# Two orders changed on VectorE: the third residual tile against a norm, and two maxima against a sum

## The chip, the cores and the metric

One core of one Trainium2 chip runs the whole program. The metric is the time on the device in microseconds (us), the median of repeated runs. A separate execution was recorded by the hardware profiler; all rows below come from it.

The names of the engines in the rows: PE is TensorE's matmul and PEld its weight load, DVE is VectorE, ACT is ScalarE, POOL is GpSimd, and SPq is the queue in which SyncE issues DMAs.

## The reference

A transformer block over x of shape (16, 512, 512): 16 batches, 512 tokens, width 512.

```python
x = x + attn(layernorm(x))     # mLSTM, 8 heads of 64 values, 32 queries/keys each
x = x + ffn(layernorm(x))      # w1, w2 made ternary, gelu, 512 -> 2048 -> 512

# one mLSTM step per head (a scan over the tokens)
m_new = max(f_log + m, i_t);  F = exp(f_log + m - m_new);  I = exp(i_t - m_new)
C = F * C + (I * k_t) v_t^T;  n = F * n + I * k_t
h = (q_t C) / (max(|q_t n|, exp(-m_new)) + EPS)
# then a norm of h over each head's 64 values, * gamma, * sigmoid(o), @ Wout.T
```

The denominator is what the second edit touches: the larger of |q n| and exp(-m), which is the larger of the three numbers q n, -q n and exp(-m).

## The kernel before

The tokens of a batch are cut into T = 4 tiles (for the scan: chunks) of 128. The scan is computed chunk by chunk: within a chunk as a masked product of scores and values, across chunks by a carried state. Matmul operands are split into a high and a low float16 part, so a product takes two or three matmuls.

**Stages.** One stage of the program, `sequence(b, fb, ahead)` on each engine, holds the attention part of batch b, the feed-forward part of batch fb = b - 1, the start of batch b + 1 (its gate product and the first values) and the first norm of batch b + 2. Every engine has its own list of instructions in program order, written out by hand; what ties the lists together are semaphores. An instruction that waits holds up all that stand behind it on its engine.

**TensorE's order at the end of a stage** (L2107 to L2137): the last quarters of the feed-forward product `down` (L1997) alternate with the output projections `project(b, t)` of the four tiles (L1840, pa<-wT,shared). After tile 2's projection come the gate product of batch b + 1 (`gates`, L1807), its first values product (`tokens`, L1840, pa<-wT,xT), and then tile 3's projection. Next come the other values products into psh, the key features (L1816), the gate columns (`gate_columns`, L1848: four small transposes that wait for ScalarE's last gate exponential, L879) and the query features. The two banks of PSUM tile `pa` are used in turn; each use waits until the one two before it has been read. The values product takes the bank that the residual of tile 2 has read; tile 3's projection takes the one that the gate sum has read.

**VectorE's order at the end of a stage** (L1623 to L1671): `head_stats` of the four chunks, with the feed-forward results (L1538) between them; the statistics of x(b+2) (`next_stats`, L1260 and L1245 to L1266); the gating of chunk 3 (L1477); and then the residuals. `residual(b, t)` adds the projection to x (L1488) and takes statistics of the sum (L1491). `next_norm` applies the norm to tiles of x(b+2) (L1271), which ScalarE and VectorE split into parts only in the next stage. `gate_sum` (L1297), `gate_minus` and `gate_logs` work on the gates of b + 1: ScalarE and VectorE take turns on them, up to ScalarE's exponentials L878 and L879.

**`head_stats(b, j, ch)`** copies the chunk's products out of PSUM (L1437 in chunk 0, L1443 in the others), makes the denominators `den` in two maxima (L1445, L1450) and two further steps (L1453, L1457), and subtracts each head's mean (sum over columns L1447, scaled by L1451, subtracted by L1455). It then gates chunk j - 1 (L1477), sums the squares that ScalarE has made (L983, L1462), and hands the variance to GpSimd (L1468). From chunk 2 on it starts only when GpSimd has finished with chunk j - 2 (L649). `den` and `norms` have 8 numbers per partition; `norms` is a strided view of the SBUF tile that the PSUM copy has written. A `Chain` gives the semaphore values for waits of VectorE on its own instructions: where an instruction reads what the one before wrote, it waits for it with `dve.wait_ge(dve_a, ch.next())`. Their number per stage is the constant DVE_A.

**GpSimd's part** in the same stretch: L637 subtracts the high part from the decays of chunks 2 and 3, `head_norm` makes the inverse square root (L642) and multiplies (L645), L649 makes the low part of the gated chunk, L599 is the root for the norm of x(b+2), and `residual_bias` (L658) makes x1b from each residual tile as soon as VectorE has written it.

Batch 0 has no feed-forward part; its stage also prepares the ternary weights (L1238, L1240). The last batch (15) has a list of its own at its end (L1639 to L1651), in which the order of the residuals is not part of the change.

Of the kernel before, what the change touches and what calls it, by code (L numbers as in the profile page):

```python
# [27 lines left out]
ALU = mybir.AluOpType  # L28
# [16 lines left out]
def at(b, per, k):  # L45

    return b * per + k
# [12 lines left out]

DVE_L, DVE_A = 3, 6 + 2 + 4 * 5 + 4 + 2 - 1 - 2
POOL_A = 4


def block_program(nc, x, Wq, Wk, Wv, Wog, Wig, big, Wfg, bfg, gamma, Wout, w1, b1, w2, b2, out):
# [48 lines left out]
    with ExitStack() as ctx:  # L116
        def sb(name, shape, dt=F32):
            return ctx.enter_context(nc.sbuf_tensor(name, shape, dt))
# [4 lines left out]
        def sem(name):  # L123
            return ctx.enter_context(nc.semaphore(name))
# [20 lines left out]
        split_scale, head_scale = sb("split_scale", [P, 2]), sb("head_scale", [P, 3])  # L145
# [101 lines left out]
        dve_l, dve_a = sem("dve_l"), sem("dve_a")  # L247
# [42 lines left out]
        def pa_bank(b, use):  # L290

            return pa_index(b, use) % 2

        def pa_filled(b, use):

            return pa_index(b, use) + 1
# [5 lines left out]
        def pa_done(b, use):  # L302

            return pa_taken(b, use) + 1
# [59 lines left out]
        def per_head(ap, n):  # L364

            return ap.rearrange("p (a h) -> p a h", h=H4).unsqueeze(3).to_broadcast([P, HG, H4, n])
# [7 lines left out]
        def by_bank(j):  # L374

            return psh[:, :, HG * (j - 1) * VA:HG * j * VA].rearrange("p h (a v) -> p a h v", a=HG)

        sum_by_group = head_sum.rearrange("p (a h) v -> p a h v", a=HG)
        heads, norms = sum_by_group[:, :, :, 0:DHV], sum_by_group[:, :, :, DHV]
# [7 lines left out]
        def by_head(ap):  # L387
            return ap.rearrange("p (a h v) -> p a h v", a=HG, h=H4)
# [726 lines left out]
        def _(dve):  # L1115
# [127 lines left out]
            def mean_var(stats, order, ch, own=slice(0, T)):  # L1243

                nc.vector.tensor_tensor(mean[:, own], stats[:, own, 1], stats[:, own, 4], ALU.add)  # L1245
                nc.vector.tensor_tensor(dif[:, own], stats[:, own, 1], stats[:, own, 4], ALU.subtract)
                nc.vector.tensor_tensor(dev[:, own], stats[:, own, 2], stats[:, own, 5], ALU.add).then_inc(order, 1)
                dve.wait_ge(order, ch.next())
                nc.vector.tensor_scalar(mean[:, own], mean[:, own], 0.5, None, ALU.mult)
                nc.vector.scalar_tensor_tensor(dif[:, own], dif[:, own], 0.25, dif[:, own], ALU.mult, ALU.mult)  # L1250
                nc.vector.tensor_scalar(dev[:, own], dev[:, own], 1.0 / D, LN_EPS, ALU.mult, ALU.add).then_inc(order, 1)
                dve.wait_ge(order, ch.next())
# [15 lines left out]
            def norm_apply(b, tiles):  # L1268
                dve.wait_ge(rstd1_ok, at(b, 1, 1))
                for t in tiles:  # L1270
                    nc.vector.tensor_scalar(xin[:, t, :], xin[:, t, :], mean[:, t:t + 1], rstd[:, t:t + 1],  # L1271
                                            ALU.subtract, ALU.mult).then_inc(xn_ok, 1)
# [150 lines left out]
            def head_stats(b, j, ch):  # L1423

                if not (isinstance(b, int) and b == 0 and j == 0):

                    dve.wait_ge(hvar_ok, at(b, T, j))
                if j >= 2:

                    dve.wait_ge(ho_lo[j - 2], at(b, 1, 1))  # L1430
                den_of = den[:, :].rearrange("p (a h) -> p a h", h=H4)

                if j == 0:
                    for g in range(HG):
                        bank = pa_bank(b, U_H0 + g)
                        dve.wait_ge(pa_fill, pa_filled(b, U_H0 + g))
                        nc.vector.tensor_copy(sum_by_group[:, g, :, :], pa[:, bank, 0:H4 * VA].rearrange("p (h v) -> p h v", v=VA)  # L1437
                                              ).then_inc(pa_free[bank], 1)
                    for g in range(HG):
                        dve.wait_ge(pa_free[pa_bank(b, U_H0 + g)], pa_done(b, U_H0 + g))  # L1440
                else:
                    dve.wait_ge(ph_fill, at(b, PH_USES, U_H + j))
                    nc.vector.tensor_copy(sum_by_group, by_bank(j)).then_inc(ph_free, 1)  # L1443
                    dve.wait_ge(ph_free, at(b, PH_USES, U_H + j))
                nc.vector.scalar_tensor_tensor(den_of, gtok[:, j, ROW_EM, :].rearrange("p (a h) -> p a h", h=H4),  # L1445
                                               head_scale[:, 0:1], norms, ALU.mult, ALU.max)
                nc.vector.tensor_reduce(hsum[:, :].rearrange("p (a h) -> p a h", h=H4), heads, AX.X,  # L1447
                                        ALU.add).then_inc(dve_a, 1)
                dve.wait_ge(dve_a, ch.next())
                nc.vector.scalar_tensor_tensor(den_of, norms, -1.0, den_of, ALU.mult, ALU.max)  # L1450
                nc.vector.tensor_scalar(hsum[:, :], hsum[:, :], 1.0 / DHV, None, ALU.mult).then_inc(dve_a, 1)  # L1451
                dve.wait_ge(dve_a, ch.next())
                nc.vector.tensor_scalar(den[:, :], den[:, :], head_scale[:, 1:2], None, ALU.add).then_inc(dve_a, 1)  # L1453
                dve.wait_ge(dve_a, ch.next())
                nc.vector.tensor_tensor(by_head(cent[j % 2]), heads, per_head(hsum[:, :], DHV),  # L1455
                                        ALU.subtract).then_inc(cent_ok, 1)
                nc.vector.scalar_tensor_tensor(den[:, :], den[:, :], head_scale[:, 2:3], den[:, :], ALU.mult, ALU.mult).then_inc(dve_a, 1)  # L1457
                dve.wait_ge(dve_a, ch.next())
                if j > 0:
                    gated(b, j - 1)  # L1460
                dve.wait_ge(sq_ok, at(b, T, j + 1))
                nc.vector.tensor_reduce(hsum[:, :], square, AX.X,  # L1462
                                        ALU.add).then_inc(dve_a, 1)
                dve.wait_ge(dve_a, ch.next())

                if not (isinstance(b, int) and b == 0 and j == 0):
                    dve.wait_ge(hn_ok, at(b, T, j))
                nc.vector.scalar_tensor_tensor(hvar[:, :], hsum[:, :], 1.0 / DHV, den[:, :], ALU.mult,  # L1468
                                               ALU.add).then_inc(hvar_ok, 1)

            def gated(b, j):
                dve.wait_ge(hn_ok, at(b, T, j + 1))
                if j == 0:
                    dve.wait_ge(sig_ok, at(b, 1, 1))

                    dve.wait_ge(qw_ok, at(b, 1, 1))
                nc.vector.scalar_tensor_tensor(cent[j % 2], cent[j % 2], H_SCALE, sig[:, j, :],  # L1477
                                               ALU.mult, ALU.mult).then_inc(gated_ok, 1)

            def residual(b, t, ch):  # L1480
                use = U_Y + t
                dve.wait_ge(pa_fill, pa_filled(b, use))
                if t == 0:
                    dve.wait_ge(res_loaded, at(b, 32, 32))
                if t == T - 1:
                    dve.wait_ge(res_last, at(b, 16, 16))
                bank, free = pa[:, pa_bank(b, use), :], pa_free[pa_bank(b, use)]
                nc.vector.scalar_tensor_tensor(xres[:, t, :], bank, evac[:, W_OUT:W_OUT + 1], xres[:, t, :],  # L1488
                                               ALU.mult, ALU.add).then_inc(free, 1)
                dve.wait_ge(free, pa_done(b, use))  # L1490
                nc.vector.bn_stats(stats[:, t, :], xres[:, t, :]).then_inc(dve_a, 1)  # L1491
                dve.wait_ge(dve_a, ch.next())
                if t == T - 1 and b < B - 1:
                    mean_var(stats, dve_a, ch)
                    nc.vector.tensor_tensor(ve[:, :], dif[:, :], dev[:, :], ALU.add).then_inc(var2, 1)
# [45 lines left out]
            def sequence(b, fb, ahead):  # L1541
                ca = Chain(b, DVE_A)
# [42 lines left out]
                def between(*qs):  # L1585
                    if not run_f:
                        for q in qs:
                            odd_unit(PLAIN + q)
# [30 lines left out]
                def next_norm(*tiles):  # L1619
                    if b + 2 < B:  # L1620
                        norm_apply(b + 2, tiles)
# [36 lines left out]
                residual(b, 0, ca)  # L1658
                between(7)
                residual(b, 1, ca)  # L1660
                next_norm(0, 1)
                residual(b, 2, ca)
                if ahead:
                    gate_sum(b + 1)
                next_norm(2, 3)
# [19 lines left out]
            for b in range(1, B - 1):  # L1685
                sequence(b, b - 1, True)
# [495 lines left out]
```

## Time and profile before

| what | value |
|---|---|
| time, median of 3 runs | 1808.9 us (1808.89 to 1809.9) |
| time of the profiled execution | 1809.62 us |
| its span, first to last instruction | 1807.9 us |
| mean granted TensorE clock | 0.986 |
| TensorE matmul busy | 1752.3 us, 97% |
| TensorE weight load busy | 878.6 us, 49% |
| VectorE busy | 1372.6 us, 76% |
| ScalarE busy | 1095.2 us, 61% |
| GpSimd busy | 622.7 us, 34% |
| DMA moved | 156.97 MB, mean 87 GB/s |

"Busy" counts the time in which an engine has an instruction in work, not how well it is used; matmuls overlap each other and their ends are modelled. A stage of a middle batch takes 106.77 us: the same instruction of the values product starts at 889.26 and at 996.03.

In the timeline rows, the end of a VectorE instruction can lie a little behind the start of the next: they overlap by some 0.08 us where the next does not wait.

### The profile page before, as it was taken

Reading aid. Unit: us, or ns where it says so; the run is one execution under the profiler, and the core shown is the slowest. Engines: PE = TensorE matmul, PEld = TensorE weight load, DVE = VectorE, ACT = ScalarE, POOL = GpSimd, SP = SyncE. Lnnn points to the kernel's source line nnn. Section 1 sums busy time; section 2 is a strip of 40 time slices with the busy share of each in tenths; the row PEclk is TensorE's granted clock in tenths of the full one; section 3 lists DMA queues with packets and bytes.
Section 4 is the critical chain, followed back from the end, with each engine's and each line's share of the span. In section 5 each row is a group of like instructions: output and inputs, shape, how many; then the busy total and the mean of one; then the engine's idle time right before and its main releaser. Section 6 shows DMA issues by size and latency. Waiting matters only on the chain.

```text
span 1807.9 us, 31974 instructions
## 1 busy us (share of the span) xinstructions
PE 1752.3 (97%) x12524; PEld 878.6 (49%) x12524; DVE 1372.6 (76%) x2450; ACT 1095.2 (61%) x1815; POOL 622.7 (34%) x481
## 2 busy tenths in 40 slices
PE   5779999999999999999999999999999999999999
PEld 3464544445454444545445454444544444454555
DVE  6786796868779686886968688686878968685772
ACT  6867648375673838557383764738476483756643
POOL 1232342524334251432525233352423425242340
PEclk8879999999999999999999999999999999999999
DMA  8525034251512525042251503325150342414020
GB/s 286 172 89 135 15 88 109 53 144 24 143 31 56 140 48 150 19 126 54 54 143 39 158 13 108 78 53 144 36 147 15 96 101 53 121 25 126 1 53 24
DMA packets 233525, 156.97 MB, mean 87 GB/s; under 512 B 195088, under 2 KB 199312, under 8 KB 228256
## 3 DMA queue, kind: packets, MB, share of 16 engines
q1 hardware_dynamic: 231792, 151.79, 31.5%
q10 hardware_dynamic: 1584, 3.15, 0.5%
q8 instruction: 99, 1.62, 0.4%
q14 instruction: 50, 0.41, 0.1%
HBM read 90.48 MB, written 17.24 MB: 60 GB/s over the span
## 4 chain that ended last, share of the span: by engine, by line
PE 70%; DVE 19%; issue 3%; POOL 2%; ACT 2%; DVEq 0%; DMA 0%; POOLq 0%; ACTq 0%
PE pf L1981 23%; PE pa L1840 14%; PE pf L1997 10%; PE pa L1816 9%; PE psh L1840 6%; DVE den L1450 3%; DVE kT L1477 2%; POOL qT L649 2%; DVE ktok L1443 2%; DVE g L1260 2%; DVE xres L1488 2%; DVE hsum L1447 2%; DVE xin L1271 1%; PE psh L1921 1%; PE psh L1898 1%
## 5 line engine op out<-in xcount | busy, mean ns | idle before, releaser
L1997 PE MATMUL pf<-w2T,gT 128*128 128x512 f16 x2048 | 497.1, 379 | 0.0
L1981 PE MATMUL pf<-x2T,w1T 128*128 128x512 f16 x1920 | 422.0, 379 | 0.0
L1531 DVE SCALAR_TENSOR_TENSOR gT<-g,wscale,gT 128x512 f16<-128x512 f32 x240 | 212.1, 884 | 213.6 <-ACT gT L978 213.0
L1981 PEld LDWEIGHTS pf<-x2T,w1T 128*128 128x128 f16 x1920 | 185.4, 98 | 222.6
L1997 PEld LDWEIGHTS pf<-w2T,gT 128*128 128x128 f16 x2048 | 195.3, 97 | 176.3
L1840 PE MATMUL pa<-wT,xT 128*128 128x512 f16 x960 | 212.9, 379 | 6.6 <-DVE xres L1488 5.5
L975 ACT ACTIVATE g<-pf,b1c 128x512 f32<-128x512 f32 x240 | 164.2, 684 | 75.5 <-PE pf L1981 73.3
L983 ACT ACTIVATE ktok<-kT 128x512 f32<-128x512 f32 x64 | 40.4, 631 | 261.9 <-DVE kT L1455 261.9
L1840 PE MATMUL pa<-wT,shared 128*128 128x512 f16 x768 | 177.8, 382 | 0.8 <-DMA shared<-qT 0.6
L978 ACT ACTIVATE gT<-g,wscale 128x512 f16<-128x512 f32 x240 | 173.2, 722 | 7.9
L1816 PE MATMUL pa<-xT,wT 128*128 128x512 f16 x768 | 172.4, 381 | 0.1
L619 POOL TENSOR_SCALAR_AFFINE_SELECT dec<-dec 128x1024 f32<-128x1024 f32 x64 | 78.3, 1223 | 260.4 <-DVE dec L1420 260.4
L942 ACT ACTIVATE dec<-dec,gtok 128x128 f32<-128x128 f32 x512 | 154.3, 390 | 0.0
L1840 PEld LDWEIGHTS pa<-wT,xT 128*128 128x128 f16 x960 | 92.6, 98 | 119.6 <-DVE xres L1488 11.8
L628 POOL TENSOR_TENSOR qw<-qw,qT 128x768 f32<-128x768 f32 x16 | 56.6, 3538 | 253.4 <-ACT sig L901 218.3
L637 POOL TENSOR_TENSOR dec<-dec 128x1024 f16<-128x1024 f32 x30 | 63.9, 2129 | 212.3 <-ACT dec L993 212.3
L1840 PE MATMUL psh<-wT,xT 128*128 128x512 f16 x576 | 126.9, 379 | 0.0
L658 POOL TENSOR_TENSOR x1b<-xres,b2r 128x512 f32<-128x512 f32 x64 | 83.0, 1306 | 117.0 <-DVE xres L1488 113.4
L642 POOL TENSOR_TENSOR hinv<-hvar,half 128x8 f32<-128x8 f32 x64 | 104.8, 1638 | 51.8 <-DVE hvar L1468 51.8
L649 POOL TENSOR_TENSOR qT<-kT,qT 128x512 f16<-128x512 f32 x64 | 73.9, 1155 | 139.2 <-ACT qT L1000 139.2
L1840 PEld LDWEIGHTS pa<-wT,shared 128*128 128x128 f16 x768 | 75.3, 98 | 92.2 <-issue 2.1
L1816 PEld LDWEIGHTS pa<-xT,wT 128*128 128x128 f16 x768 | 74.8, 98 | 87.8 <-issue 1.6
(232 smaller groups left out, 2704.9 us busy)
## 6 DMA issues: line engine op xcount, KB each, us to landing
dec<-gate_r SPq DMA_DIRECT2D x32, 1024.0 KB, 5.6
xin<-L_attn_x SPq DMA_DIRECT2D x16, 1024.0 KB, 5.5
out<-x1b SPq DMA_DIRECT2D x64, 256.0 KB, 2.2
xres<-L_attn_x SPq DMA_DIRECT2D x16, 512.0 KB, 5.9
xres<-L_attn_x SPq DMA_DIRECT2D x32, 256.0 KB, 3.0
qw<-gate_w SPq DMA_DIRECT2D x128, 48.0 KB, 5.7
gT<-L_ffn_w SPq DMA_DIRECT2D x5, 1024.0 KB, 4.8
gT<-L_ffn_w ACTq DMA_DIRECT2D x3, 1024.0 KB, 7.0
```

What stands on the lines that cost most here:

```text
L619: nc.gpsimd.affine_select(out=rows_of, in_=rows_of, compare_op=ALU.is_ge, fill=0.0, base=0, pattern=[[0, 2 * T], [1, P]], channel_multipli ...
L642: nc.gpsimd.tensor_tensor(hinv[:, :], hvar[:, :], half[:, :], ALU.pow).then_inc(pool_a, 1)
L649: nc.gpsimd.tensor_tensor(head_parts[j % 2][:, LO, :], cent[j % 2], head_parts[j % 2][:, HI, :], ALU.subtract).then_inc(ho_lo[j], 1)
L658: nc.gpsimd.tensor_tensor(x1b[:, t, :], xres[:, t, :], b2r[:, :], ALU.add).then_inc(x1b_ok, 1)
L942: last = nc.scalar.activation(dec[:, h, tok(j)], dec[:, h, tok(j)], ACT.Exp, bias=gtok[:, j, ROW_C, h:h + 1])
L975: nc.scalar.activation(g32[:, f % 2, :], pf[:, use % 2, :], ACT.Gelu, bias=b1c[:, f:f + 1], scale=1.0 / X_SCALE).then_inc(pf_free[use % 2], 1)
L978: nc.scalar.activation(gT[:, HI, f, :], g32[:, f % 2, :], ACT.Copy, scale=wscale[:, W_GELU:W_GELU + 1]).then_inc(g_hi, 1)
L1531: nc.vector.scalar_tensor_tensor(gT[:, LO, f, :], g32[:, f % 2, :], wscale[:, W_GELU:W_GELU + 1], gT[:, HI, f, :], ALU.mult, ALU.subtract) ...
L1816: last = nc.tensor.matmul(bank, wT[:, ws, k, col:col + P], xT[:, xs, :, k, :], start=(k == 0 and n == 0), stop=(k == KD - 1 and n == 2))
L1840: last = nc.tensor.matmul(bank, src[:, xs, k, :], wT[:, ws, k, col:col + D], start=(k == 0 and n == 0), stop=(k == KD - 1 and n == 2))
L1981: last = nc.tensor.matmul(bank, w1T[:, k, tok(f)], x2T[:, part, :, k, :], start=(k == 0 and part == HI), stop=(k == KD - 1 and part == LO))
L1997: last = nc.tensor.matmul(bank, gT[:, part, f, tok(t)], w2T[:, f, :], start=(f == 0 and part == HI), stop=(f == NF - 1 and part == LO), sk ...
```

## The change

```diff
-DVE_L, DVE_A = 3, 6 + 2 + 4 * 5 + 4 + 2 - 1 - 2
+DVE_L, DVE_A = 3, 6 + 2 + 4 * 6 + 4 + 2 - 1 - 2
...
                 nc.vector.scalar_tensor_tensor(den_of, gtok[:, j, ROW_EM, :].rearrange("p (a h) -> p a h", h=H4),
-                                               head_scale[:, 0:1], norms, ALU.mult, ALU.max)
+                                               head_scale[:, 0:1], norms, ALU.mult, ALU.max).then_inc(dve_a, 1)
+                dve.wait_ge(dve_a, ch.next())
+                nc.vector.scalar_tensor_tensor(den_of, norms, -1.0, den_of, ALU.mult, ALU.max)
                 nc.vector.tensor_reduce(hsum[:, :].rearrange("p (a h) -> p a h", h=H4), heads, AX.X,
                                         ALU.add).then_inc(dve_a, 1)
                 dve.wait_ge(dve_a, ch.next())
-                nc.vector.scalar_tensor_tensor(den_of, norms, -1.0, den_of, ALU.mult, ALU.max)
                 nc.vector.tensor_scalar(hsum[:, :], hsum[:, :], 1.0 / DHV, None, ALU.mult).then_inc(dve_a, 1)
...
                 residual(b, 1, ca)
+                residual(b, 2, ca)
                 next_norm(0, 1)
-                residual(b, 2, ca)
                 if ahead:
                     gate_sum(b + 1)
                 next_norm(2, 3)
```

In `head_stats`, the second maximum (L1450) moves ahead of the sum over columns (L1447). It reads what the first one wrote, and nothing stands between them now, so it waits for it: one wait of VectorE on itself more per chunk, which is what DVE_A counts. In VectorE's `sequence`, the residual and statistics of tile 2 move ahead of the norm of the first two tiles of x(b+2). No instruction is added or taken away, and no other engine's list changes.

## Rows read from the trace of the kernel before

**Rows 1.** The page, its first part: busy time of each engine.
```profile
PE 1752.3 (97%) x12524; PEld 878.6 (49%) x12524; DVE 1372.6 (76%) x2450; ACT 1095.2 (61%) x1815; POOL 622.7 (34%) x481
```

**Rows 2.** Waits of PE, whole span: who for whom, us, times, longest.
```profile
PE pa L1840 <- DVE xres L1488: 5.5, 13, 0.5
```

**Rows 3.** Timeline of PE: start, us, instruction, count, idle before it.
```profile
991.43 2.75 PE L1840 MATMUL pa<-wT,shared 128*128 128x512 f16 x12
...
996.03 2.76 PE L1840 MATMUL pa<-wT,xT 128*128 128x512 f16 x12 [0.43 <-DVE xres L1488]
```

**Rows 4.** Timeline of DVE, 990 to 998 us.
```profile
990.31 0.74 DVE L1488 SCALAR_TENSOR_TENSOR xres<-pa,evac,xres 128x512 f32<-128x512 f32 x1
...
992.61 0.69 DVE L1491 BATCH_NORM_STATS2 stats<-xres 128x6 f32<-128x512 f32 x1
993.34 1.97 DVE L1271 TENSOR_SCALAR xin<-xin,mean,rstd 128x512 f32<-128x512 f32 x2
995.24 0.74 DVE L1488 SCALAR_TENSOR_TENSOR xres<-pa,evac,xres 128x512 f32<-128x512 f32 x1
996.01 0.69 DVE L1491 BATCH_NORM_STATS2 stats<-xres 128x6 f32<-128x512 f32 x1
996.74 0.68 DVE L1297 TENSOR_TENSOR qT<-pa,qT 40x512 f32<-40x512 f32 x1
997.35 0.99 DVE L1271 TENSOR_SCALAR xin<-xin,mean,rstd 128x512 f32<-128x512 f32 x2
```

**Rows 5.** Timeline of POOL, same stretch.
```profile
992.35 2.68 POOL L658 TENSOR_TENSOR x1b<-xres,b2r 128x512 f32<-128x512 f32 x2
996.05 1.27 POOL L658 TENSOR_TENSOR x1b<-xres,b2r 128x512 f32<-128x512 f32 x1 [1.02 <-DVE xres L1488]
```

**Rows 6.** Groups of DVE, 994.4 to 995.3 us: busy us, mean ns.
```profile
L1271 DVE TENSOR_SCALAR xin<-xin,mean,rstd 128x512 f32<-128x512 f32 x1 | 1.5, 1487 | 0.0
```

**Rows 7.** Timelines of ACT, PEld and PE at the gate columns.
```profile
1013.06 0.52 ACT L879 ACTIVATE stack<-sig 8x384 f32<-8x384 f32 x1
1013.96 0.49 PEld L1848 LDWEIGHTS psh<-ident,stack 72*128 72x128 f32 x4
1014.17 0.42 PE L1848 MATMUL psh<-ident,stack 72*128 72x72 f32 x4
```

**Rows 8.** Timelines of DVE, POOL and ACT, chunks 0 and 1, 959 to 970 us.
```profile
959.00 0.23 DVE L1445 SCALAR_TENSOR_TENSOR den<-gtok,head_scale,ktok 128x8 f32<-128x8 f32 x1
959.09 2.13 POOL L637 TENSOR_TENSOR dec<-dec 128x1024 f16<-128x1024 f32 x1 [13.73 <-ACT dec L993]
959.86 1.38 DVE L1450 SCALAR_TENSOR_TENSOR den<-ktok,den 128x8 f32<-128x8 f32 x1
961.63 0.69 DVE L1455 TENSOR_TENSOR kT<-ktok,hsum 128x512 f32<-128x512 f32 x1
965.76 1.04 POOL L645 TENSOR_TENSOR kT<-kT,hinv 128x512 f32<-128x512 f32 x1
966.11 1.04 ACT L993 ACTIVATE dec<-dec 128x1024 f16<-128x1024 f32 x1
966.79 0.23 DVE L1445 SCALAR_TENSOR_TENSOR den<-gtok,head_scale,ktok 128x8 f32<-128x8 f32 x1
967.23 2.13 POOL L637 TENSOR_TENSOR dec<-dec 128x1024 f16<-128x1024 f32 x1 [0.42 <-ACT dec L993]
969.76 0.69 DVE L1455 TENSOR_TENSOR kT<-ktok,hsum 128x512 f32<-128x512 f32 x1
```

**Rows 9.** Timelines of POOL and DVE, batch 1, chunk 2.
```profile
227.53 1.08 POOL L645 TENSOR_TENSOR kT<-kT,hinv 128x512 f32<-128x512 f32 x1
227.53 0.17 DVE L1450 SCALAR_TENSOR_TENSOR den<-ktok,den 128x8 f32<-128x8 f32 x1
227.62 1.02 DVE L1451 TENSOR_SCALAR hsum<-hsum 128x8 f32<-128x8 f32 x1
```

**Rows 10.** Timelines of POOL, DVE and PE, batch 0.
```profile
112.66 1.04 POOL L645 TENSOR_TENSOR kT<-kT,hinv 128x512 f32<-128x512 f32 x1
113.37 0.35 DVE L1445 SCALAR_TENSOR_TENSOR den<-gtok,head_scale,ktok 128x8 f32<-128x8 f32 x1
127.74 0.27 PE L1760 MATMUL pf<-ident,x2T 128*128 128x128 f16 x1 [5.43 <-DVE x2T L1240]
```

**Rows 11.** Timeline of PE, last batch.
```profile
1742.04 1.06 PE L1959 MATMUL psh<-ident,xres 128*128 128x128 f32 x8 [0.61 <-DVE xres L1508]
```

## The prediction

> **What bounds the kernel.** I read the page first: TensorE is busy for 97% of the span, VectorE for 76% [rows 1]. So time can only come out of gaps on TensorE or out of the few places where TensorE is not full. The waits of TensorE come next: between the first and the last batch there is only one kind, its values product for the next batch (L1840, pa<-wT,xT) waiting for VectorE's residual (L1488), 13 times, 5.5 us in all [rows 2]. Then the timeline of one period. Batches repeat every 106.77 us, so I work on the one around 990 us; others differ by hundredths. TensorE is gapless but for 0.43 us ahead of 996.03 [rows 3]. It waits there for the bank that the residual of tile 2 frees at 995.24 + 0.74 = 995.98, while VectorE spent 993.34 to 995.31 on the norm of two tiles of x(b+2) [rows 4]. That is the gap which the moved residual aims at.
>
> **Part 1, what goes.** With the residual of tile 2 first, it starts when its projection is done: 991.43 + 2.75 = 994.18 [rows 3], plus some 0.1, so about 994.3, and the bank is free near 995.0, half a microsecond before TensorE asks (996.03 - 0.43 = 995.60). The gap goes in 13 stages: 13 x 0.43 = 5.5 us at most. The norm is not called for b = 14 and 15, and batch 0 has no such gap. GpSimd's x1b of tile 2 is issued earlier too; no DMA moves.
>
> **Part 2, what that brings.** VectorE now idles until 994.3, then does residual and statistics (0.77 + 0.73 start to start [rows 4]), then the two norm tiles, and only then the gate sum (L1297). Everything depends on how long those two tiles take. Alone, two take 0.99 us; the pair at 993.34 took 1.97 [rows 4], its second tile 1.49 [rows 6]. What stretched it is GpSimd: its two x1b ran 992.35 to 995.03 [rows 5], and the norm tile ended 0.28 us after. The same collision comes back. GpSimd's x1b of tile 2 starts now as soon as residual 2 and the two before it are done, about 995.1, and runs 1.27 us; the first norm tile arrives at 995.8, inside it. It ends 0.28 us behind x1b, at 996.6, the second 0.45 later. The gate sum starts at 997.0 instead of 996.74: 0.26 us later (before counting part 3). Bounds: 996.75 (no collision, shift 0) and, if part 3 makes GpSimd late as well, 997.2 and more.
>
> Who waits for the gate sum? TensorE's last projection takes the bank it frees; it reaches that near 998.2, the sum ends by 997.9, so no wait. But VectorE has no idle time from there to the last gate operand, so the shift runs through to ScalarE's last gate exponential (L879), which ended at 1013.06 + 0.52 = 1013.58. TensorE's gate-column transposes (L1848) loaded their weights at 1013.96 and ran at 1014.17 [rows 7]. The slack is therefore 0.33 us at the weight load, counting 0.05 for the signal (995.98 to 996.03 [rows 3, 4]). TensorE now comes 0.3 to 0.4 us earlier and the exponential 0.26 or more later: **the wait moves from the values product to the gate columns**. The gain of a stage is what is left: with load start to transpose between 0 and 0.21 us, transposes start at 1013.58 + shift + 0.05 + (0 to 0.21). For a shift of 0.26 that is 1013.89 to 1014.10, gain 0.28 to 0.07.
>
> **Part 3, the maxima.** L1450 works on 8 elements per row and yet took 1.38 us in chunk 0: started 959.86, ended 961.24, where GpSimd's decay subtraction (L637) ran 959.09 to 961.22 [rows 8]. Its twin L1445, issued at 959.00, just ahead of GpSimd, took 0.23. So two SBUF inputs on VectorE wait for GpSimd. In one stage L1450 slipped in ahead and then L1451, one input, took the wait: 1.02 us, to the end of GpSimd's L645 [rows 9]. Both kinds can be held; L1447, the sum over columns, never is (it ran under L637 here).
>
> The Trainium skill, page "SBUF — State Buffer", section "Who interferes with whom", has the same as a rule: VectorE and GpSimd share a port pair, the first to start holds it for its whole instruction, reductions stay out of it. By that rule, which the trace agrees with, this edit does harm wherever GpSimd has already begun.
>
> Now each chunk in the new order, per period:
> - Chunk 0: L1450 wants to start at 959.26, after GpSimd's 959.09. Held to 961.24. The sum over columns, earlier hidden under the hold, now follows: 0.61 + 0.10 for its wait = 0.71 us later at L1455 (961.63 to 962.34). ScalarE's copy of dec (966.11) is queued behind the squares and the sigmoids, so it shifts 0.71 too, and L637 of the next chunk with it (967.23 to 967.94); L645 moves from 965.76 to 966.47 [rows 8].
> - Chunk 1: its copy is set by TensorE, so L1445 still wants 966.79, but L645 now holds it to 967.53. L1450 at 967.56 gets in ahead of L637; the sum is done at 968.33; L1451 is held by L637 to 967.94 + 2.13 = 970.07. L1455 at 970.40 instead of 969.76 [rows 8]: 0.64 late.
> - Chunks 2 and 3: each starts when GpSimd's L649 of two chunks before ends, so the delay is handed on; L1450 is clear of the hold, L1451 takes it instead. Saved: 0.08 each (L1450 ended at GpSimd's end and L1451 came behind it; now L1451 ends there). 0.48 is left at residual 0.
>
> Bounds of this: if L1450 of chunk 0 gets in at 959.26 the shift is -0.1 to -0.3; if nothing is won back, +0.71. I take 0.48, since the hold of [rows 8] is the same instruction pair 0.6 us later.
>
> Effect: residual 0 frees its bank at 990.31 + 0.74 + 0.48 = 991.53, and TensorE wants it by 991.43 [rows 3, 4]: stall 0.15. x1b 0 starts 992.83, x1b 2 at 992.83 + 2 x 1.22 = 995.27, ends 996.54; norm tiles end 996.82 and 997.27; gate sum 997.20, shift **0.46**. Transposes at 1014.09 to 1014.30, against 1014.17: a stage changes by -0.08 to +0.13, middle +0.02, 13 stages: +0.3 us (-1.0 to +1.7).
>
> **The two ends.** In batch 0 GpSimd collides little (L1445 once took 0.35, to the end of L645), and VectorE's chunk work lies on the path: TensorE stood 5.43 us before 127.74 for VectorE's L1240 [rows 10]. The new wait behind L1445 costs 0.26 - 0.15 = 0.11 us (start to start with a wait: 0.23 + 0.03; without, the next instruction starts 0.08 before the end), three chunks after TensorE's last say: +0.3. In the last batch chunks 1 to 3 and residuals lie on the path too (TensorE idled 0.61 us for the norm L1508 [rows 11]): +0.5, the shift above. The skill's page "VectorE: DVE Perf Modes", section "The DRAIN you can't avoid", says a semaphore between VectorE instructions costs nothing extra. The rows' starts say 0.11 here; by the page the batch-0 term would be 0 and the total 0.3 lower.
>
> **Sum.** +0.3 + 0.3 + 0.5 = +1.1 us on the profiled execution's 1809.62 (span 1807.9 and 1.7 around it), 1810.7; that execution lies 0.7 above the median of 1808.9, so 1810.0.
>
> **Rivals.**
> - The order of the maxima is harmless (L1450 of chunk 0 gets in). Then shift 0.26, gain 0.07 to 0.28 in 13 stages, 0.9 to 3.6, less 0.3 in batch 0: about 1807. For it: L645 and L1450 started together and once VectorE won [rows 9]. Against: here GpSimd has 0.17 us of lead.
> - Faster: the norm tiles do not collide and the gate exponential is in time. The 5.5 us stay, less 0.8 for the ends: 1804.2. For it: the next pair of norm tiles was undisturbed (997.35, 0.99). Against: that one started just as x1b ended (996.05 + 1.27).
> - Slower: the gate columns become a longer wait than the one removed. It decides from a shift of about 0.33 to 0.54; if nothing is won back in chunks 2 and 3 (0.7 at residual 0), the gate sum comes 0.68 late, transposes at 1014.36 + 0.1, 0.29 x 13 = 3.8, plus 1.0 at the ends: 1813.7. For it: VectorE has no idle time in which a delay is absorbed. Against: [rows 9] show the saving behind a held L1451.
> - The change doesn't do what it says: the values product still waits, for another reason (the gate product's own end). 1809.5.
>
> **Chances.** Forecast 0.55, harmless maxima 0.15, faster 0.13, slower 0.15, no effect 0.02. A measurement of this kernel tells some 0.2% (3.6 us) from no change. Faster by over that: 0.14; slower: 0.15 and the forecast's tail, 0.17; within: 0.69. The range runs into both outer cases: 1804.0 to 1812.8; the forecast's own is 1808.7 to 1811.5.
>
> **What would show it.** TensorE's wait for L1488 ahead of L1840 gone, and one for ScalarE (L879) at L1848 in its place, or near it; L1450 in chunk 0 near 2 us and in the others 0.17; L1451 near 1 us in chunks 2 and 3; period still 106.7 to 106.9. A period of 106.4 would make me wrong on the gate path, one above 107.1 wrong on its size; a short L1450 in chunk 0 wrong on who holds the port.

## The result and the profile after

| | before | after |
|---|---|---|
| median of 20 runs each | 1809.99 us | 1812.54 us |
| lowest to highest | 1808.26 to 1811.57 | 1811.04 to 1814.55 |
| ratio after / before, 95% interval | | 1.0016 [1.0010, 1.0022] |
| profiled execution, its span | 1809.62, 1807.9 | 1812.49, 1810.8 |
| one stage of a middle batch | 106.77 | 106.87 to 106.99 |

The change makes the kernel slower by 0.16%, 2.9 us (the two medians differ by 2.55). That is small, but the interval does not hold 1. The forecast was 1.1 us and "no change". The runs of one kernel scatter by some 3 us with TensorE's granted clock (those of after with a mean of 0.985 or 0.986 took 1811.04 to 1813.07 us, those with 0.983 or 0.984 took 1813.65 to 1814.55), so medians are compared by ratio to runs of the kernel before taken beside them.

Each kernel has one profiled execution, and every time inside a stage below is read from it; the middle stages of one kernel mostly repeat each other within 0.1 us, and the exceptions are named. In both profiles the granted clock of TensorE is below full speed only in the first 142 us (0.73 in before and 0.61 in after from 115 to 130 us, 1.00 from 142 us on).

The diff adds one line ahead of most places, so L1450 of before is L1448 now, L1447 is L1449, L1451 is L1452, and everything behind has its old number plus one (L1488 is L1489, L1840 is L1841, L1848 is L1849). L879 and L637 stay. At the stage of [rows 3], after runs 1.67 us behind before (the transposes one stage earlier start at 909.07 against 907.40), so 1.67 is taken off whenever a time of after is set against one of before.

Waits of TensorE from 250 to 1700 us, the whole answer (who for whom, us, times, longest), which answers to [rows 2] (before has the first of its 13 waits just ahead of 250 us):

```profile
PE psh L1849 <- ACT stack L879: 2.4, 13, 0.2
PE pa L1841 <- DMA shared<-qT: 0.5, 3, 0.2
```

The 5.5 us for the residual are gone, and 2.4 us of a wait for ScalarE's gate exponential have come: the list alone says that 2.6 us were won. It does not show all. The timelines of PE, its weight loads, and VectorE of after (start, us, instruction, count, idle before it), answering to [rows 3] and [rows 4]:

```profile
989.68 3.62 PE L1998 MATMUL pf<-w2T,gT 128*128 128x512 f16 x16
993.39 2.75 PE L1841 MATMUL pa<-wT,shared 128*128 128x512 f16 x12
996.07 1.49 PE L1808 MATMUL pa<-xT,wgT 128*64 128x512 f16 x12
997.49 2.76 PE L1841 MATMUL pa<-wT,xT 128*128 128x512 f16 x12
```

```profile
993.36 2.29 PEld L1841 LDWEIGHTS pa<-wT,shared 128*128 128x128 f16 x12 [0.56 <-issue]
```

```profile
992.49 0.74 DVE L1489 SCALAR_TENSOR_TENSOR xres<-pa,evac,xres 128x512 f32<-128x512 f32 x1
...
996.24 0.75 DVE L1489 SCALAR_TENSOR_TENSOR xres<-pa,evac,xres 128x512 f32<-128x512 f32 x1 [0.76 <-PE pa L1841]
997.03 0.69 DVE L1492 BATCH_NORM_STATS2 stats<-xres 128x6 f32<-128x512 f32 x1
997.76 1.32 DVE L1271 TENSOR_SCALAR xin<-xin,mean,rstd 128x512 f32<-128x512 f32 x2
999.00 0.67 DVE L1297 TENSOR_TENSOR qT<-pa,qT 40x512 f32<-40x512 f32 x1
```

The values product follows the gate product 1.42 us later (996.07 to 997.49), where before it took 1.91 (994.12 to 996.03): this gap is closed, as meant. But tile 2's projection follows the sixteen matmuls ahead of it 3.71 us later (989.68 to 993.39), where before it took 3.45 (987.98 to 991.43). That stall of 0.26 us is in no wait list: the matmul has no bracket, and the weight load's idle time stands there as "issue". The reason can be read off: idle time is counted from the modelled end of the matmul ahead (989.68 + 3.62 = 993.30), and that end lies 0.17 us behind the start of a successor that waits for nothing (3.62 against 3.45), so only 0.09 is left, and it is not listed. One finds the stall only by the distance of two starts in both traces. It ends 0.16 us after residual 0 (992.49 + 0.74 = 993.23) frees the bank.

The gate columns, timelines of ACT and PE, answering to [rows 7]:

```profile
1015.30 0.52 ACT L879 ACTIVATE stack<-sig 8x384 f32<-8x384 f32 x1
```

```profile
1010.45 5.34 PE L1817 MATMUL pa<-xT,wT 128*128 128x512 f16 x24
1015.97 0.44 PE L1849 MATMUL psh<-ident,stack 72*128 72x72 f32 x4 [0.18 <-ACT stack L879]
```

Here, too, the cost is more than the bracket: 5.52 us from start to start against 5.18 before (1008.99 to 1014.17), so 0.34, while the list says 0.18.

Chunks 0 and 1 in VectorE's and GpSimd's timelines, answering to [rows 8]:

```profile
960.69 0.23 DVE L1445 SCALAR_TENSOR_TENSOR den<-gtok,head_scale,ktok 128x8 f32<-128x8 f32 x1
960.96 1.98 DVE L1448 SCALAR_TENSOR_TENSOR den<-ktok,den 128x8 f32<-128x8 f32 x1
962.87 0.67 DVE L1449 TENSOR_REDUCE hsum<-ktok 128x8 f32<-128x512 f32 x1
...
964.05 0.69 DVE L1456 TENSOR_TENSOR kT<-ktok,hsum 128x512 f32<-128x512 f32 x1
...
968.48 0.76 DVE L1445 SCALAR_TENSOR_TENSOR den<-gtok,head_scale,ktok 128x8 f32<-128x8 f32 x1
969.28 0.17 DVE L1448 SCALAR_TENSOR_TENSOR den<-ktok,den 128x8 f32<-128x8 f32 x1
...
970.08 1.72 DVE L1452 TENSOR_SCALAR hsum<-hsum 128x8 f32<-128x8 f32 x1
972.10 0.69 DVE L1456 TENSOR_TENSOR kT<-ktok,hsum 128x512 f32<-128x512 f32 x1
...
976.38 0.23 DVE L1445 SCALAR_TENSOR_TENSOR den<-gtok,head_scale,ktok 128x8 f32<-128x8 f32 x1
976.64 0.17 DVE L1448 SCALAR_TENSOR_TENSOR den<-ktok,den 128x8 f32<-128x8 f32 x1
...
977.44 0.86 DVE L1452 TENSOR_SCALAR hsum<-hsum 128x8 f32<-128x8 f32 x1
```

```profile
960.78 2.14 POOL L637 TENSOR_TENSOR dec<-dec 128x1024 f16<-128x1024 f32 x1 [13.73 <-ACT dec L993]
968.18 1.04 POOL L645 TENSOR_TENSOR kT<-kT,hinv 128x512 f32<-128x512 f32 x1
969.65 2.13 POOL L637 TENSOR_TENSOR dec<-dec 128x1024 f16<-128x1024 f32 x1 [0.42 <-ACT dec L993]
...
975.51 1.64 POOL L642 TENSOR_TENSOR hinv<-hvar,half 128x8 f32<-128x8 f32 x1
```

The second maximum works on 8 elements of a row and takes 1.98 us: it ends at 962.94, 0.02 behind GpSimd's L637, and the sum over columns, which used to run under that hold, comes behind it. In the later chunks it takes 0.17, and L1452 is held in its place: 1.72 us in chunk 1, 0.86 in chunk 2. Not every GpSimd instruction holds VectorE: in chunks 2 and 3 of 15 stages both maxima, with two SBUF inputs each, ran inside GpSimd's L642, which reads only 8 numbers per partition, and took their 0.23 and 0.17 us as if alone.

Where the 2.9 us lie: the same ScalarE instruction, the first one that reads a batch's gate sums from PSUM (L852), splits the span.

| stretch | before | after | difference | forecast |
|---|---|---|---|---|
| start to batch 1's L852 | 142.00 | 142.43 | +0.43 | +0.3 |
| fourteen stages, to batch 15's L852 | 1494.31 | 1496.31 | +2.00 | +0.3 |
| from there to the end | 171.59 | 172.06 | +0.47 | +0.5 |

```profile
142.43 0.59 ACT L852 ACTIVATE qT<-pa 40x512 f32<-40x512 f32 x1 [0.34 <-PE pa L1808]
...
1638.74 0.59 ACT L852 ACTIVATE qT<-pa 40x512 f32<-40x512 f32 x1 [4.70 <-PE pa L1808]
```

The end came as forecast, and other kernels bear it out: from L852 to the end, the four with the old maxima (before, residual alone, norm split, gate sum first) take 171.56 to 171.62, the three with the new ones in all chunks (after, maxima alone, maxima and split) 172.03 to 172.07. The start cannot be counted as confirmed: the same four kernels with the old maxima reach batch 1's L852 at 142.00 to 144.34, so that 0.43 is far inside what this stretch scatters between profiled executions, and its nearness to the forecast may be luck. The middle did not come as forecast.

### The profile page after: what moved, and what is told of

It is laid out like the page before. It is cut to its first block, busy times and chain, and to the rows that moved or that the text cites. A ratio compares the mean times of both kernels' runs of the same rounds, so it can differ in the third digit from the quotient of the medians.

```text
span 1810.8 us, 31974 instructions
## 1 busy us (share of the span) xinstructions
PE 1756.6 (97%) x12524; PEld 876.1 (48%) x12524; DVE 1380.6 (76%) x2450; ACT 1093.3 (60%) x1815; POOL 620.3 (34%) x481
## 4 chain that ended last, share of the span: by engine, by line
PE 71%; DVE 16%; issue 4%; ACT 3%; DMA 2%; POOL 1%; SPq 0%; DVEq 0%; POOLq 0%; ACTq 0%
PE pf L1982 23%; PE pf L1998 18%; PE pa L1841 15%; PE pa L1817 5%; DMA shared<-qT 2%; DVE xin L1271 1%; PE psh L1922 1%; PE psh L1938 1%; PE psh L1899 1%; DVE xres L1489 1%; DVE hsum L1452 1%; DVE stats L1492 1%; PE psh L1972 1%; POOL qT L649 1%; DVE g L1337 1%
## 5 line engine op out<-in xcount | busy, mean ns | idle before, releaser
L1841 PE MATMUL pa<-wT,xT 128*128 128x512 f16 x960 | 212.9, 380 | 1.0 <-ACT sig L901 0.9
L1841 PE MATMUL pa<-wT,shared 128*128 128x512 f16 x768 | 177.8, 382 | 2.5 <-DMA shared<-qT 1.5
L1841 PEld LDWEIGHTS pa<-wT,xT 128*128 128x128 f16 x960 | 92.5, 98 | 113.3 <-issue 6.2
L637 POOL TENSOR_TENSOR dec<-dec 128x1024 f16<-128x1024 f32 x30 | 63.9, 2131 | 212.3 <-ACT dec L993 212.3
L1841 PE MATMUL psh<-wT,xT 128*128 128x512 f16 x576 | 126.9, 380 | 0.0
L642 POOL TENSOR_TENSOR hinv<-hvar,half 128x8 f32<-128x8 f32 x64 | 104.8, 1638 | 62.6 <-DVE hvar L1469 62.6
L1841 PEld LDWEIGHTS pa<-wT,shared 128*128 128x128 f16 x768 | 74.0, 98 | 97.3 <-issue 7.3
```

The lines of the kernel that those rows point to most:

```text
L642: nc.gpsimd.tensor_tensor(hinv[:, :], hvar[:, :], half[:, :], ALU.pow).then_inc(pool_a, 1)
L1841: last = nc.tensor.matmul(bank, src[:, xs, k, :], wT[:, ws, k, col:col + D], start=(k == 0 and n == 0), stop=(k == KD - 1 and n == 2))
```

## The experiments

The seven take the middle's term apart. The first four share their runs of the kernel before (median 1810.12 us), and so do the last three (1810.22).

**Residual alone.** Before, with residual 2 ahead of the norm and the maxima left in their old order.

```diff
                 residual(b, 1, ca)
+                residual(b, 2, ca)
                 next_norm(0, 1)
-                residual(b, 2, ca)
```

> Only the residual of tile 2 is moved ahead of the norm; the maxima stand as before. Theory (the maxima are what turned the gain into a loss): nothing is late at residual 0, TensorE's wait of 0.43 us at the values product goes, the first norm tile is still held by GpSimd's x1b, the gate sum comes some 0.28 us later and the gate columns start 0.15 us behind ScalarE's L879, at 1014.0 of the period around 990 instead of 1014.17. Period 106.6 instead of 106.77, 13 x 0.16 = 2.1 us faster than before. Rival (the moved residual itself does the harm): slower by 2 to 3 us, as with the whole change.

Measured: 1808.56 us, ratio 0.9993 [0.9984, 1.0002], stage 106.64. TensorE's only wait in the middle is the one for L879 at the gate columns, 2.4 us in 13 times, as in after. The moved residual by itself is worth 0.13 us a stage, 1.66 us over fourteen (1492.65 against 1494.31). It trades 0.49 for 0.34. The time came out 1.6 us below before where 2.1 were expected, and its interval still holds 1; what shows the gain is the sum of the stages.

**Maxima alone.** After, with residual 2 back behind the norm.

```diff
                 residual(b, 1, ca)
-                residual(b, 2, ca)
                 next_norm(0, 1)
+                residual(b, 2, ca)
```

> Only the second maximum is moved ahead of the sum over columns; the residual of tile 2 stays behind the norm. Theory: chunk 0's second maximum is held by GpSimd's L637, 0.48 us are left at the residuals, and with the old order each stage's values product waits for residual 2, so the whole 0.48 us goes into the period: 107.25, 13 x 0.48 + 0.9 at the ends = 7 us slower than before. Rival (TensorE hides what happens in the chunks): within 1 us of before, and the 2 us of the whole change then come from the moved residual.

Measured: 1815.97, ratio 1.0038 [1.0026, 1.0051], stage 107.25, as expected to the hundredth. The fourteen stages take 6.3 us more than before (1500.63 against 1494.31). The maxima alone cost 0.48 a stage, as much as residual 0 is late: 0.25 at tile 2's projection (993.07 to 996.77, 3.70) and the rest at the values product, whose wait grows from 0.43 to 0.66:

```profile
PE pa L1841 <- DVE xres L1489: 8.2, 13, 0.7
PE pa L1841 <- DMA shared<-qT: 0.5, 3, 0.2
```

**Chunk 0's maximum back.** After, with the second maximum of chunk 0 alone behind the sum over columns again; the other chunks keep the new order. The diff is cut at the dots.

```diff
...
+                if j > 0:
+                    first_max.then_inc(dve_a, 1)
+                    dve.wait_ge(dve_a, ch.next())
+                    nc.vector.scalar_tensor_tensor(den_of, norms, -1.0, den_of, ALU.mult, ALU.max)
...
                 dve.wait_ge(dve_a, ch.next())
+                if j == 0:
+                    nc.vector.scalar_tensor_tensor(den_of, norms, -1.0, den_of, ALU.mult, ALU.max)
```

> The whole change, but in chunk 0 the second maximum stays behind the sum over columns (the first two instructions need no wait between them there). Theory (it is chunk 0's hold by L637 that makes the rest late): L1455 of chunk 1 comes within 0.1 us of before, chunks 2 and 3 win 0.08 each, residual 0 is early, and the kernel is as fast as with the residual alone: 2 us faster than before. Rival (the added wait in every chunk does it): some 0.1 to 0.2 us per chunk remain, and it is slower than before by 1 to 2 us.

Measured: 1808.41, ratio 0.9990 [0.9981, 0.9999], stage 106.65, the same as with the residual alone. Only chunk 0's order does harm; tile 2's projection is back at 3.45 us. One stage of the thirteen, the last of the middle, is the exception: its period is 106.98, residual 0 is late there, and this time the wait is long enough to be listed:

```profile
1525.09 2.75 PE L1845 MATMUL pa<-wT,shared 128*128 128x512 f16 x12 [0.19 <-DVE xres L1493]
```

```profile
1524.20 0.74 DVE L1493 SCALAR_TENSOR_TENSOR xres<-pa,evac,xres 128x512 f32<-128x512 f32 x1
```

Why residual 0 is late in that one stage was not looked into.

**The norm split around the residual.** Before, with one norm tile put where VectorE otherwise waits for tile 2's projection, and the second behind it.

```diff
                 residual(b, 1, ca)
-                next_norm(0, 1)
+                next_norm(0)
                 residual(b, 2, ca)
+                next_norm(1)
```

> The maxima as before; one norm tile ahead of the residual of tile 2 and one behind it. Theory (the gate sum's delay is what takes the gain away): the first norm tile fits into the 0.7 us in which VectorE would idle for the projection, the second is held by x1b to about 996.6, the gate sum starts at 996.6, 0.1 to 0.2 us earlier than before, and the gate columns make no one wait. All of the 0.43 us stays: period 106.34, 13 x 0.43 = 5.6 us faster than before. Rival (something else late in the stage binds once that wait is gone): no better than the residual alone, 2 us faster.

Measured: 1803.50, ratio 0.9965 [0.9953, 0.9978], stage 106.28. Its list of TensorE's waits from 250 to 1700 us is empty. VectorE and the gate columns:

```profile
992.25 0.56 DVE L1271 TENSOR_SCALAR xin<-xin,mean,rstd 128x512 f32<-128x512 f32 x1
993.14 0.75 DVE L1488 SCALAR_TENSOR_TENSOR xres<-pa,evac,xres 128x512 f32<-128x512 f32 x1 [0.32 <-PE pa L1841]
993.92 0.69 DVE L1491 BATCH_NORM_STATS2 stats<-xres 128x6 f32<-128x512 f32 x1
994.65 0.87 DVE L1271 TENSOR_SCALAR xin<-xin,mean,rstd 128x512 f32<-128x512 f32 x1
995.45 0.68 DVE L1297 TENSOR_TENSOR qT<-pa,qT 40x512 f32<-40x512 f32 x1
```

```profile
1011.75 0.52 ACT L879 ACTIVATE stack<-sig 8x384 f32<-8x384 f32 x1
```

```profile
1007.41 5.34 PE L1817 MATMUL pa<-xT,wT 128*128 128x512 f16 x24
1012.59 0.42 PE L1849 MATMUL psh<-ident,stack 72*128 72x72 f32 x4
```

One norm tile fits ahead of the residual; with it gone from behind, the gate exponential ends at 1012.27, 0.32 before the transposes, which start 5.18 us behind their forerunner, the shortest distance in any of these kernels. This is the fastest version of all.

**The gate sum ahead of three norm tiles.** As the last, but with residual 2, then the gate sum, and then the other three norm tiles.

```diff
-                next_norm(0, 1)
+                next_norm(0)
                 residual(b, 2, ca)
                 if ahead:
                     gate_sum(b + 1)
-                next_norm(2, 3)
+                next_norm(1, 2, 3)
```

> As the split norm (maxima as before, one norm tile ahead of the residual of tile 2), but the gate sum comes directly behind that residual and the three other norm tiles behind it. Theory: the split norm already left TensorE without a wait, at its own work of 106.3 us a period, so an earlier gate sum buys nothing: 0 to 0.5 us from the split norm, 6 us faster than before; the norm tiles then run free of x1b, the gate operands end no later than before. Rival (there is still something to gain from the gates): faster than the split norm by 1 us or more.

Measured: 1804.92, ratio 0.9975 [0.9966, 0.9983], stage 106.40. It was expected within 0.5 us of the norm split and is 1.4 us slower by the medians; their intervals overlap, but the sum of the fourteen stages says the same (1489.49 against 1487.88, 1.6 us). The gate sum comes only 0.19 us sooner behind residual 2 (993.24 to 995.36, against 993.14 to 995.45 in the split), since it waits for ScalarE's L852, and the three norm tiles stand ahead of the next gate operand:

```profile
995.36 0.68 DVE L1297 TENSOR_TENSOR qT<-pa,qT 40x512 f32<-40x512 f32 x1 [0.64 <-ACT qT L852]
995.97 1.44 DVE L1271 TENSOR_SCALAR xin<-xin,mean,rstd 128x512 f32<-128x512 f32 x3
```

The transposes start 5.29 us behind their forerunner (1007.51 to 1012.80), 0.11 more than with the split.

**New maxima with the split norm.** This isolates the stall that the maxima leave when the gate columns are in time.

```diff
                 residual(b, 1, ca)
+                next_norm(0)
                 residual(b, 2, ca)
-                next_norm(0, 1)
+                next_norm(1)
```

> The new maxima of the change, with the norm split around the residual of tile 2. Theory (of the 2 us lost in the middle stages most is TensorE's stall for residual 0, whose price I had too low: 0.27 us instead of 0.15): the stall at tile 2's projection stays, with no wait at the values product or the gate columns; period 106.28 + 0.27 = 106.55, with 0.9 at the ends 2 us faster than before, 4.4 slower than the split norm with the old maxima. Rival (the stall is hidden by what follows once the gates are in time): within 1 us of the split norm.

Measured: 1808.33, ratio 0.9993 [0.9984, 1.0002], stage 106.56: 0.28 over the split with the old maxima, as expected. VectorE's residual 0, and TensorE:

```profile
991.91 0.74 DVE L1489 SCALAR_TENSOR_TENSOR xres<-pa,evac,xres 128x512 f32<-128x512 f32 x1
```

```profile
989.08 3.62 PE L1999 MATMUL pf<-w2T,gT 128*128 128x512 f16 x16
992.80 2.75 PE L1842 MATMUL pa<-wT,shared 128*128 128x512 f16 x12
```

The projection comes 3.72 us behind its forerunner, 0.27 late, and again 0.15 behind the end of residual 0 (992.65). With the old maxima the distance is 3.46 (986.89 to 990.35). So this stall, which no wait list names, is the whole cost of the maxima in this stage when the gate columns are in time.

**Chunk 0's norms from PSUM.** After, with chunk 0's second maximum reading the norms from the two PSUM banks, in two instructions, so that only one of its inputs is in SBUF; the banks are given back by it and not by the copies. The diff is cut at the dots.

```diff
...
+                if j == 0:
+                    for g in range(HG):
+                        bank = pa_bank(b, U_H0 + g)
+                        own = pa[:, bank, 0:H4 * VA].rearrange("p (h v) -> p h v", v=VA)[:, :, DHV]
+                        nc.vector.scalar_tensor_tensor(den_of[:, g, :], own, -1.0, den_of[:, g, :], ALU.mult,
+                                                       ALU.max).then_inc(pa_free[bank], 1)
...
```

> The whole change, but in chunk 0 the second maximum reads the norms from the two PSUM banks instead of their copy in SBUF (two instructions of 4 numbers per row, one SBUF input each; the banks are freed behind them, which TensorE needs much later). Theory (what is held by GpSimd is the second SBUF input): both take 0.1 to 0.25 us while GpSimd's L637 runs, chunk 0 is 0.1 to 0.2 late instead of 0.71, and the kernel is 1 to 2 us faster than before. Rival (any small VectorE instruction issued behind GpSimd's start is held): they take 2 us as in the change, and the kernel stays 2 to 3 us slower than before.

Measured: 1811.75, ratio 1.0006 [0.9997, 1.0015], stage 106.65. The first part came true. VectorE and GpSimd:

```profile
961.91 0.23 DVE L1452 SCALAR_TENSOR_TENSOR den<-pa,den 128x4 f32<-128x4 f32 x2
962.06 0.68 DVE L1456 TENSOR_REDUCE hsum<-ktok 128x8 f32<-128x512 f32 x1
962.77 1.20 DVE L1459 TENSOR_SCALAR hsum<-hsum 128x8 f32<-128x8 f32 x1
```

```profile
961.81 2.13 POOL L637 TENSOR_TENSOR dec<-dec 128x1024 f16<-128x1024 f32 x1 [13.73 <-ACT dec L993]
```

Both halves of the second maximum run inside GpSimd's L637 and are not held; what is held is the next instruction that can be, the scaling of the sums. The head norm of chunk 0 starts 3.09 us behind the second copy out of PSUM (961.18 to 964.27), against 3.16 before and 3.89 after, so all of chunk 0's delay is gone. The Trainium skill, page "SBUF — State Buffer", section "Who interferes with whom", lets a VectorE instruction contend when both its inputs are in SBUF; this run agrees: 0.23 us for the pair from PSUM against 1.98 for one from SBUF.

The second part missed: the run was to be 1 to 2 us faster than before, and is not, by an interval that holds 1. The stages' sum is 1493.2, 1.1 less than before (with one stage of 107.12 among those of 106.65), and the end takes 171.26 against 171.59, but batch 1's L852 comes at 145.54 instead of 142.00. In batch 0, TensorE waits for the bank that the maximum now holds longer (first line), and the granted clock of 95 to 105 and 105 to 115 us is 0.50 and 0.67, where the run with chunk 0's maximum back had 0.63 and 0.88. The windows' columns are stretch, us, busy time of PE, PEld, DVE, ACT and POOL, granted clock, DMA share and GB/s.

```profile
PE pa L1724 <- DVE den L1452: 1.1, 1, 1.1
```

```profile
95.00:105.00 10.00, 8.90 (x83) 8.42 (x82) 6.30 (x16) 9.14 (x13) 2.34 (x2) 0.50 0.29 111
105.00:115.00 10.00, 8.45 (x56) 8.25 (x52) 5.52 (x13) 2.92 (x6) 1.95 (x3) 0.67 0.01 2
```

A clock of 0.50 is the 1.2 GHz level. The wait is not needed to bring it: the profiled executions of five kernels that have no such wait (residual alone, maxima alone, norm split, gate sum first, maxima and split) show the same 0.50 and 0.67 in these two stretches. They reach batch 1's L852 at 143.59 to 144.37. So this kernel's start is 1.2 us or more behind that of others with the same low clock. The wait of 1.1 us is of that size, but no run here has it alone. What brings the low clock in some executions stays open.

## Why the prediction was wrong

**One table settles the middle.** In the stage around 990 us three distances on TensorE differ between the kernels, each read as the difference of two starts: A, the sixteen matmuls to tile 2's projection; B, the gate product to the values product; C, the last query product to the gate columns' transposes. The norm split has all three at their shortest.

| kernel | A | B | C | 106.28 + what exceeds the split's | stage measured |
|---|---|---|---|---|---|
| norm split | 3.46 | 1.42 | 5.18 | | 106.28 |
| before | 3.45 | 1.91 | 5.18 | 106.76 | 106.77 |
| after | 3.71 | 1.42 | 5.52 | 106.87 | 106.90 |
| residual alone | 3.46 | 1.42 | 5.52 | 106.62 | 106.64 |
| maxima alone | 3.70 | 2.15 | 5.18 | 107.25 | 107.25 |
| chunk 0 back | 3.45 | 1.42 | 5.52 | 106.61 | 106.65 |
| gate sum first | 3.45 | 1.42 | 5.29 | 106.38 | 106.40 |
| maxima and split | 3.72 | 1.41 | 5.18 | 106.53 | 106.56 |
| norms from PSUM | 3.45 | 1.41 | 5.54 | 106.62 | 106.65 |

Nine kernels add up to within 0.04 us: nothing else in this stage moved.

**Part 1, right.** B closes (1.41 or 1.42) in every kernel in which residual 2 stands ahead of at least one of the two norm tiles.

**Part 2, right.** The wait moved to the gate columns, as the residual alone shows. Two norm tiles took 1.32 us through the collision with x1b, ending 0.14 later than worked out (999.08 - 1.67 = 997.41 against 997.27), and the exponential's end to the transposes is 0.15 us, the middle of the 0.05 to 0.26 taken.

**Part 3, right in its mechanism.** Chunk 0's hold, 0.71 late at its head norm (964.05 - 1.67 = 962.38, forecast 962.34), chunk 1's (970.43 against 970.40), the hold that L1452 takes in its place, and the delay left at residual 0 (992.49 - 1.67 - 990.31 = 0.51, forecast 0.48) all came within 0.06 us. That the second SBUF input is what lets L637 hold a maximum was borne out, and then shown by the run from PSUM. What the prediction did not say is that it depends on the GpSimd instruction: L642 held neither maximum in chunks 2 and 3.

**The step that failed** is the sentence "TensorE wants it by 991.43: stall 0.15". The delay in it was right and the slack too large. The bank's release reached TensorE's matmul 0.15 to 0.16 us after the residual's end, in three kernels (after 993.23 to 993.39, maxima alone 996.62 to 996.77, maxima and split 992.65 to 992.80), and again in the one listed wait of the run with chunk 0's maximum back (1524.94 to 1525.09). It is not the transposing DMA of that tile's chunk that TensorE waits for: in after it was issued at 989.00 and landed 3.1 us later, 1.1 before residual 0's end. I had taken 0.05 from the values product in [rows 3, 4], where the same step does take 0.05 to 0.06. So the slack at the projection was 991.43 - 0.15 - 991.05 = 0.23 us (991.05 is residual 0's end in before), and of the half microsecond of delay 0.26 stayed as a stall. Why one handover takes 0.15 and the other 0.05 stays open. The extra 0.11 then runs through, as the prediction said a delay would: projection, residual 2, x1b 2, norm, gate sum (999.00 - 1.67 = 997.33, forecast 997.20), exponential (1014.15, forecast 1014.04), transposes (1014.30 against 1014.17 before). A late stage is +0.13, the upper end of the -0.08 to +0.13 given, and not the +0.02 I put into the sum. Over 13 stages the difference of 0.11 is 1.4 of the missing 1.7 us.

**What I had not seen** is the rest. In the first six stages with a norm, up to 800 us, the stall lies one tile earlier, and the six periods from gate columns to gate columns (160.46 to 802.16) sum to 641.70, 0.30 above six of 106.90. The upper ones, 106.97 to 106.99, lie above the 106.7 to 106.9 that the prediction gave as its sign. Timelines of PE and of the issuing DMA queue, after:

```profile
341.89 3.62 PE L1998 MATMUL pf<-w2T,gT 128*128 128x512 f16 x16
345.67 2.77 PE L1841 MATMUL pa<-wT,shared 128*128 128x512 f16 x12 [0.15 <-DMA shared<-qT]
```

```profile
340.77 1.30 SPq L541 DMA_TRANSPOSE shared<-qT  x1
```

Tile 1's projection comes 3.78 us behind its forerunner, 0.33 late: chunk 1, itself half a microsecond late, is transposed by this DMA, which landed 4.8 us after its issue, just 0.10 before the matmul starts. Tile 2's projection, 348.27 being its forerunner's start, is then on time (3.45). At 983.63 the same place is on time (3.46) and the 0.26 falls on tile 2. A stage pays at one or the other, and more where it pays at tile 1. Which of the two it is goes with the DMA: that of chunk 1 landed 4.8 or 4.9 us after its issue in all six early stages and 3.1 to 3.7 us after it in the seven later ones, and in the run with the maxima alone it took 4.8 or 4.9 in the five stages that pay at tile 1 and at most 4.0 in the others. In before, the same six DMAs took 3.1 to 4.0. Why six of them took longer in after stays open. The prediction moved GpSimd and ScalarE with the late chunks but did not follow the chunk's own output through its DMA to its reader. With the two, +0.3 becomes 0.3 + 1.4 + 0.3 = 2.0, as measured.

**The rivals.** "Harmless maxima" and "faster" fell with chunk 0's 1.98 us and with the collision. "Slower", by gate columns that wait longer than the wait removed, gave +4.8 (1813.7 on 1808.9) and is about as far from the measured 2.9 as the forecast's 1.1, but its cause is refuted: C costs 0.34, still less than the 0.49 won at B. What turned the balance is A. The forecast's +0.02 was a gain of 0.43 less two losses, 0.15 at A and some 0.30 at C, that together came to as much; 0.11 us of error in one of them, 13 times over, was five times the sum that it was put at.

## What to carry to other kernels

Moving a short VectorE operation earlier is not free when it has two SBUF inputs: look at what GpSimd starts just before it (L637 and L645 held it here, L642 did not), since the reorder can put a tiny instruction, and all the work behind it, at the end of a 2 us hold. When a wait is removed, measure the slack of the next two consumers by distances of starts rather than by the wait list, and take each handover from that very edge; of the 0.60 us that TensorE loses in a stage of after, at A and C, the list names 0.18. And put one piece of filler into the idle time ahead of a late operation instead of moving the whole block behind it: one tile in front and one behind gained 6.6 us (1810.12 to 1803.50), where both behind gained 1.6, by its interval at the edge of what could be told from nothing.

## What the runs showed that was not expected

- The handover from VectorE to a TensorE matmul through a freed bank took 0.05 to 0.06 us at the values product and 0.15 to 0.16 at tile 2's projection.
- One transposing DMA of a stage landed 4.8 to 4.9 us after its issue in six stages and 3.1 to 3.7 in the next seven, and so moved the stall from one tile to another.
- A wait between two tiny VectorE instructions costs 0.11 us from start to start (0.27, 960.69 to 960.96, against 0.15 to 0.16 without it, as in before and in the run with chunk 0's maximum back). The Trainium skill, page "VectorE: DVE Perf Modes", section "The DRAIN you can't avoid", has it cost nothing, for long copies; here the trace differs.
- The effects of the two parts do not add: alone they are -0.13 and +0.48 a stage, together +0.13 where the sum would be +0.35. Half of the maxima's cost lies at B (1.91 to 2.15), and with the residual moved B stays closed (1.42), so only the half at A is paid.
